# Splitting GpSimd's three wide rounding steps into halves, and planning with other durations, in a one-core transformer layer

## The reference

```python
x = x + attention(layernorm(x), Wq, bq, Wk, bk, Wv, bv, Wo, bo)   # x: 2 x 2048 x 256, 16 heads of 16, causal, rope
x = x + ffn(layernorm(x), w_gate, w_up, w_down)                    # inner width 704

def fp4_quant_dequant(x):            # blocks of 16 along the last dim
    scale = max(max(abs(block)) / 6, 1e-12)
    return grid(block / scale) * sign * scale      # grid 0, .5, 1, 1.5, 2, 3, 4, 6
def fp4_linear(x, w): return fp4_quant_dequant(x) @ fp4_quant_dequant(w).T
def ffn(x):           return fp4_linear(silu(fp4_linear(x, w_gate)) * fp4_linear(x, w_up), w_down)
```

## Time and profile before

| what | before |
|---|---|
| median of 3 runs | 1327.4 us (1326.84 to 1329.7) |
| the profiled execution | 1327.12 us, its span 1324.8 us |
| PE busy | 1235.4 us, 93% of the span |
| DVE busy | 1079.2 us, 81% |
| ACT busy | 773.1 us, 58% |
| POOL busy | 474.7 us, 36% |

### The profile page before, as it was taken

One profiled execution on the slowest core, in us unless ns is written; L12 is line 12 of the kernel. 1 busy time (PEld: TensorE's weight loads), 2 busy tenths in 40 slices (PEclk: granted clock), 3 DMA queues, 4 the chain that ended last, 5 costly groups with the idle time before them and its releaser, 6 DMA issues.

```text
span 1324.8 us, 43878 instructions
## 1 busy us (share of the span) xinstructions
PE 1235.4 (93%) x18934; PEld 712.9 (54%) x18934; DVE 1079.2 (81%) x2434; ACT 773.1 (58%) x1659; POOL 474.7 (36%) x500
## 2 busy tenths in 40 slices
PE   7568899999999999999989899999999999999967
PEld 6445555554555545555546655555555546545445
DVE  5778988978988899899618788899899898994356
ACT  5335566655656446567675456557566585776621
POOL 2956625645231131311106554313213121023346
PEclk9778999999999999999999999999999999999979
DMA  4623322222011000110122312120111100000000
GB/s 107 169 75 103 86 70 58 66 65 58 11 33 35 26 18 11 33 26 11 36 65 59 89 42 58 42 51 10 35 34 35 35 2 19 3 3 17 14 13 16
DMA packets 63901, 57.54 MB, mean 43 GB/s; under 512 B 17359, under 2 KB 57297, under 8 KB 63697
## 3 DMA queue, kind: packets, MB, share of 16 engines
q1 hardware_dynamic: 60680, 53.67, 15.4%
q10 hardware_dynamic: 3028, 1.09, 0.3%
HBM read 37.55 MB, written 16.78 MB: 41 GB/s over the span
## 4 chain that ended last, share of the span: by engine, by line
PE 71%; DVE 16%; POOL 5%; issue 3%; ACT 3%; DMA 2%; SPq 0%; ACTq 0%; POOLq 0%; DVEq 0%
PE bank L911 16%; PE bank L865 14%; PE bank L887 14%; PE bank L923 11%; DVE piece_max L1270 6%; PE bank L1036 5%; PE bank L983 3%; ACT prob L1172 2%; PE bank L1027 2%; PE bank L991 1%; PE bank L918 1%; DVE c_mem L1347 1%; PE bank L998 1%; PE bank L892 1%; DVE c_mem L1337 1%
## 5 line engine op out<-in xcount | busy, mean ns | idle before, releaser
L1172 ACT ACTIVATE prob<-bank 128x512 f32<-128x512 f32 (+3 forms) x1280 | 603.7, 539 | 272.8 <-PE bank L887 150.6
L1270 DVE TENSOR_REDUCE piece_max<-bank 128x1 f32<-128x512 f32 (+14 forms) x1280 | 675.6, 579 | 26.5 <-PE bank L865 13.6
L887 PE MATMUL bank<-q_mem,k_mem 99*32 99x512 bf16 (+15 forms) x5120 | 397.6, 341 | 8.6 <-DVE piece_max L1270 5.2
L865 PE MATMUL bank<-k_mem,q_mem 96*32 96x512 bf16 (+14 forms) x5120 | 388.5, 343 | 6.7 <-DVE piece_max L1270 4.3
L911 PE MATMUL bank<-prob,V 128*32 128x512 f32 (+3 forms) x2560 | 296.2, 534 | 12.2 <-ACT prob L1172 11.7
L1484 POOL TENSOR_TENSOR c_mem<-c_mem 128x256 f32<-128x256 f32 (+2 forms) x74 | 86.4, 1168 | 443.8 <-DVE c_mem L1359 443.8
L887 PEld LDWEIGHTS bank<-q_mem,k_mem 99*32 99x32 bf16 x5120 | 144.6, 96 | 159.1 <-issue 77.3
L865 PEld LDWEIGHTS bank<-k_mem,q_mem 96*32 96x32 bf16 x5120 | 143.4, 97 | 144.7 <-issue 81.8
L892 PE MATMUL bank<-mask_kq,ident_h 128*32 128x128 bf16 (+3 forms) x2048 | 104.8, 201 | 0.0
L911 PEld LDWEIGHTS bank<-prob,V 128*32 128x32 f32 x2560 | 67.8, 110 | 63.6 <-ACT prob L1172 26.3
L870 PE MATMUL bank<-mask_qk,ident_h 128*32 128x32 bf16 x2048 | 93.9, 182 | 0.0
(11 more groups left out here) (173 smaller groups left out, 1390.1 us busy)
## 6 DMA issues: line engine op xcount, KB each, us to landing
parts_dram<-a_mem SPq DMA_DIRECT2D x13, 512.0 KB, 4.0
q_mem<-parts_dram SPq DMA_DIRECT2D x32, 192.0 KB, 3.0
k_mem<-parts_dram SPq DMA_DIRECT2D x32, 192.0 KB, 3.5
q_mem<-parts_dram SPq DMA_DIRECT2D x32, 128.0 KB, 3.0
k_mem<-parts_dram SPq DMA_DIRECT2D x32, 128.0 KB, 3.4
c_mem<-in_L_attn_x SPq DMA_DIRECT2D x30, 128.0 KB, 2.1
out<-c_mem SPq DMA_DIRECT2D x30, 128.0 KB, 1.7
a_mem<-in_L_attn_x SPq DMA_DIRECT2D x13, 256.0 KB, 3.0
```

What stands on the lines that cost most here:

```text
L865: m = pe.matmul(b[COLUMNS * h:COLUMNS * (h + 1), of], q_rows(u)[0:TERM_ROWS, h, block * COLUMNS:(block + 1) * COLUMNS], k_rows(k0 // CHUNK ...
L887: mm = pe.matmul(b[k0:k0 + COLUMNS, since:CHUNK], k_rows(j // TPC, g)[:, h, first:first + COLUMNS], q_rows(u)[:, h, since:CHUNK], start=Tr ...
L1172: act.activation(prob[:, n % NP, off:CHUNK], bank_of("st", n)[:, off:CHUNK], ACT.Exp, scale=SCALE).then_inc(drained("st", n)[0], 1)
L1270: r = dve.tensor_reduce(piece_max[:, u % 2, block, slot:slot + 1], bank_of("s1", n)[:, column:column + keys], AX.X, ALU.max)
```

## The change

GpSimd's three rounding steps on rows of 704 become six, each on a half of 352 numbers, ordered add/add, subtract/subtract, multiply/multiply. Rows of 256 stay whole. What TensorE waits for is still the last of them. Two waits move: the q matmuls wait for q's weight alone and the k matmuls for k's (both waited for both), and in rope the step that overwrites the memory which the v matmuls still read comes third, so that the first two steps do not wait for v. All else alters only the planner's assumptions, and through them the order of the streams.

```diff
-DMA_TURN_NS, DMA_NS, DMA_KB_PER_NS, DIVIDE_NS, BESIDE_NS = 460, 1500, 0.2, 96, 2000
-SOONER_NS = dict(a=0, w=0, xn=10000, s=200, st=0, pv=-100, place=1000, norm=200, c=(0, -2000), tile=1000)
+DMA_TURN_NS, DMA_NS, DMA_KB_PER_NS, DIVIDE_NS, JOIN_NS, BESIDE_NS = 460, 1500, 0.2, 96, 150, 2500
+SOONER_NS = dict(a=0, w=0, xn=10000, s=200, st=0, pv=-1000, place=10000, norm=200, c=(0, -2000), tile=1000)
...
         if engine == "pe" and divided != self.divided:
-            ns, self.divided = ns + DIVIDE_NS, divided
+            ns, self.divided = ns + (DIVIDE_NS if divided else JOIN_NS), divided
...
+        if engine == "pool" and self.sharing[0] <= begin < self.sharing[1]:
+            ns += self.sharing[1] - begin
+        if shares:
+            self.sharing = begin, begin + ns
...
-        for n, ns in enumerate((whole, 85, blocks / 2, whole, whole / 2, whole / 2)):
-            yield from plan.step("dve", ("round", n) + key, ns, last, shares=n in (1, 4, 5))
+        for n, ns in enumerate((whole, 90, 62 + 0.39 * width, whole, whole / 2 + 36, whole / 2 + 36)):
+            yield from plan.step("dve", ("round", n) + key, ns, last, shares=n in (1, 3, 4, 5))
...
-        for n in range(3):
-            yield from plan.step("pool", ("grid", n) + key, 150 + (2.1 if n < 2 else 1.7) * width, last)
+        halves = grid_halves(width)          # 2 for rows of 704, else 1
+        for n, half in itertools.product(range(3), range(halves)):
+            yield from plan.step("pool", ("grid", n, half) + key, 150 + (2.1 if n < 2 else 1.7) * width / halves,
+                                 [("grid", n - 1, half) + key] if n else last)
...
             def project_features(b, z, o):
-                for s in range(2):
-                    at.wait_ge(*drained("aw", s))
+                at.wait_ge(*drained("aw", o))
...
-            at.wait_ge(*filled("v", z))
-            engine.tensor_tensor(to[:, :, 0], qk[:, :, 0], cos, ALU.mult).then_inc(done, 1)
-            yield when["rope1", z]
...
             engine.tensor_tensor(temp[:, 0], qk[:, :, 1], sin, ALU.mult).then_inc(done, 1)
+            yield when["rope1", z]
+            engine.tensor_tensor(temp[:, 1], qk[:, :, 0], sin, ALU.mult).then_inc(done, 1)
             yield when["rope2", z]
+            at.wait_ge(*filled("v", z))
+            engine.tensor_tensor(to[:, :, 0], qk[:, :, 0], cos, ALU.mult).then_inc(done, 1)
...
+                for n, half in itertools.product(range(3), range(halves)):
+                    at_, of = slice(half * each, (half + 1) * each), slice(half * nb, (half + 1) * nb)
+                    a, b, to = v["qa"][0:rows, at_], v["qb"][0:rows, at_], dst[:, at_]
+                    yield when[("grid", n, half) + key]
+                    if n == 0:
+                        at.wait_ge(*rounded)
+                        pool.tensor_tensor(a, a, b, ALU.add).then_inc(done, 1)
+                    elif n == 1:
+                        at.wait_ge(done, first + half + 1)
+                        pool.tensor_tensor(a, a, b, ALU.subtract).then_inc(done, 1)
+                    else:
+                        at.wait_ge(done, first + halves + half + 1)
+                        pool.tensor_tensor(...)      # multiply by the blocks' scales
```

More of the change, by code:

```diff
@@ L82, in __init__ @@
         self.spare, self.bank_free = list(banks), {b: 0.0 for b in banks}
-        self.jobs, self.now, self.running, self.moved, self.divided = [], 0.0, None, 0.0, False
+        self.jobs, self.now, self.running, self.moved = [], 0.0, None, 0.0
+        self.divided, self.sharing = False, (0.0, 0.0)
     def start(self, job, sooner=0.0):
@@ L306, in rehearse_projection @@
         for o, name in enumerate(("q", "k")):
[L307 to L308 removed]
+            plan.start(plan.through((name, z), 1728, "act", 360,
+                                    [("drain", "xnT", z), ("drain", "aw", o)],
                                     [("drain", "bias")] + old("lo"),
[L310 removed]
+                                    ("act", (name + "0", z), 372, ("drain", "bias"), *old("lo"))), pair_sooner(z))
         plan.start(plan.through(("v", z), 1728, "dve", 600, [("drain", "xnT", z), ("drain", "aw", 2)],
@@ L317, in rehearse_projection @@
         rope, ns = ("dve", 600) if rope_on_vector(z) else ("pool", 1235)
-        for n, after in enumerate(([("drain", "q", z), ("drain", "k", z), ("drain", "table", z), ("v", z)], old("stored", len(STORES) - 1),
-                                   [], [], [("rope1", z)], [("rope3", z)])):
-            yield from plan.step(rope, (f"rope{n}", z), ns, after)
+        for n, after in enumerate(([("drain", "q", z), ("drain", "k", z), ("drain", "table", z)] + old("stored", len(STORES) - 1),
+                                   [], [("v", z)], [], [("rope2", z)], [("rope3", z)])):
+            yield from plan.step(rope, (f"rope{n}", z), ns, after, shares=rope == "dve")
         yield from plan.step("act", ("hi", z), 960, [("rope5", z)])
-        yield from plan.step(rope, ("rest", z), 1130 if rope_on_vector(z) else 2200, [("hi", z)])
+        yield from plan.step(rope, ("rest", z), 1130 if rope_on_vector(z) else 2120, [("hi", z)], shares=rope == "dve")
         plan.start(rehearse_parts(z), pair_sooner(z))
@@ L330, in rehearse_low_part @@
     def rehearse_low_part(z):
[L331 removed]
+        yield from plan.step("dve", ("lo", z), 1135, [("mid", z)], shares=True)
         for n in range(1, len(STORES)):
@@ L433, in rehearse_weights @@
                 yield from rehearse_rounding(("w", n), width, ready)
-                ready = [("grid", 2, "w", n)]
+                ready = [("grid", 2, grid_halves(width) - 1, "w", n)]
             for part in range(weight_parts[n]):
-                yield from plan.through(("fw", n, part), 330, "act", 480, ready + [("ident load",)])
+                yield from plan.through(("fw", n, part), 330, "act", 300 + 190 * (name == "d" and part == 0), ready + [("ident load",)])
                 yield from plan.wait([("drain", "fw", n, part)])
```

72 lines of the change are left out of this document (30 added, 42 removed).

## The result

The changed kernel takes 1312.2 us (median of 4 runs, 1310.8 to 1314.0) where the kernel before takes 1327.1 us (4 runs, 1326.5 to 1329.7): the ratio is 0.9883, with a 95% interval of 0.9870 to 0.9895. That is 15 us less, where 7.6 us less were forecast. The direction is right and the time lies in the range, but the gain is twice the one that was forecast, so the working has to be gone through term by term. The profiled execution took 1312.96 us with a span of 1311.2 us; before it was 1324.8.

A forecast was written before the change was run, and what follows sets the result against it. TensorE was taken as nine tenths busy or more in nearly all of the middle, with holes at both ends. Terms -1.3 - 0.9 - 3.4 - 2.0 = -7.6 us took 1327.4 to 1319.8 us, range 1309 to 1330.

The forecast's parts named there:

- The end: Last tiles' chain: VectorE waits less behind halved GpSimd steps, 1.95 us back less 0.67 for the halves: -1.3 us.
- the price of the halves: GpSimd's wide roundings: six half steps cost 0.67 us more than three whole ones, 0.53 by spacing of starts.
- Rope: At the start, VectorE's first two rope steps run ahead of v's matmuls: -0.9 us.
- The moved waits of the weights: First q matmul, at the start: the wait for the k weight may cost at most 0.3 us, counted as nothing.
- The placing: First unit, before its second pass: fewer row maxima between its steps, -3.4 us; first exponential before 82.
- The mode changes: TensorE's full stretch: 20 fewer of 334 changes at 0.10 us each, -2.0 us.
- the values product's bias: TensorE's values product yields to scores up to 1 us younger; counted as nothing, hidden by TensorE's queue.
- the other assumed durations: Planner's durations: change only the order, which can't be priced; counted as nothing, they widen the range.
- Starved weights: Rival, at the start: sooner placing delays the weights' rounding and TensorE waits, +6.0 us, 1333; chance 0.17.
- Start repaired: Rival: better durations remove two of TensorE's three waits for weights, -17.8 us at most, some 1311; chance 0.16.
- GpSimd held up: Rival, last three tiles: VectorE gets in at the halves' new borders, the end gives +3.2, 1324.3 us; chance 0.08.
- GpSimd busy 497 us: Sign over the whole kernel: 34 wide roundings at 0.67 us make GpSimd busy 23 us more, 497 us.

The follow-up runs named there:

- e1: The changed kernel with its planned order kept, GpSimd's three wide steps emitted whole where their first halves stood: 1318.5 us, ratio 0.9944.
- e12: The kernel before in its own order, with GpSimd's three wide steps cut into halves in place: 1327.9 us, ratio 0.9989.
- e7: The kernel before with only the three new biases (BESIDE_NS 2500, pv -1000, place 10000): 1308.4 us, ratio 0.9850.
- e16: The order of e7, with GpSimd's wide steps cut into halves in place: 1309.2 us, ratio 0.9848 against the kernel before.
- e17: The changed kernel with the biases whose plan had the earliest rehearsed end of 300 (BESIDE_NS 2750, pv -1000, place 1000, s 250): 1290.6 us, ratio 0.9707.
- e8: The changed kernel with all three biases set back to their old values: 1338.1 us, ratio 1.0074 against the kernel before.
- e11: The kernel before with BESIDE_NS at 2050 instead of 2000, a change that means nothing: 1344.0 us, ratio 1.0121.
- e5: The changed kernel with 151 added two-column matmuls of the whole array in the first pass, 574 mode changes: 1368.8 us, ratio 1.0297.
- e6: Control for e5: the changed kernel with four tiny strip matmuls at each of the same 151 places, 302 mode changes: 1313.6 us, ratio 0.9889.

## Why the prediction was half right

- **The end, -1.3.** The mechanism is right: VectorE waits for the rest of a shorter step, and at a fixed order the end gains 1.8 us (e1) or 2.3 us (e12). Mis-sized was the price of the halves, 0.19 us a rounding for 0.67: -1.95 + 0.19 = -1.8. The prediction came nearest with 0.53, where it took start-to-start spacing into account. But the kernel's end gained nothing, 63.4 to 63.7 us, since the new order of the last tiles gave back about 2 us (e1's 65.5 against 63.4). I had reckoned the end in the old order's chain, and there left out the c_mem tile between the two k_mem tiles, whose lines 1347 and 1355 (1.66 and 1.28 us) lie on it too.
- **Rope, -0.9.** The start moved from 19.73 to 18.84, as forecast, but the sixth step ends only 0.24 us sooner and the first store is no sooner. The term counted the start and not what VectorE puts in between. It was not tried alone, and rope's first step starts anywhere from 18.6 to 20.3 us in the kernels of the old type, so 0.9 us of one execution say little.
- **The moved waits of the weights, 0.** q's matmuls start at 11.87 us, ahead of the second weight's transposes, instead of at 13.04; k's last drain starts at 18.24 instead of 18.27. Nothing came of it, as forecast; not tried alone.
- **The placing, -3.4.** 8.7 us instead of 7.5, so 2.3 us gained there; the first exponential at 77.2 met its mark of 82. The loss in the first 100 us fell by 1.7 to 2.8 us, where 4.3 were forecast for rope and placing together. Sixes of row maxima became twos, but two of VectorE's steps on 16 numbers still took 1.32 and 2.09 us.
- **The mode changes, -2.0.** 32 fewer instead of 20, at a confirmed 0.10 us: 3.2 us. A right price, a number too low.
- **The step that failed** is the sentence beside it: the values product's bias counted nothing, "hidden by TensorE's own queue", and "the other assumed durations change only the order, which I can't price; they count nothing and widen the range". The middle was worth -12 us where the sum had -2.0. With the three biases alone, at the old durations and with whole steps, e7 gains 20 us, more than the whole change and far more than the 5.4 us that the sum gave to placing and mode changes: the order, which the sum put at nothing, was its largest term. About 3 of the 12 us are mode changes; by e1 some 2.5 are the halves in this order (e12 and e16 show that the same halves give nothing there in two others); the rest is not taken apart by a run. Fewer waits for exponentials are among it (9 for 20 in the middle), longer waits for the placed maxima stand against it (6.5 us for 1.0). The shares of the parts stay open, since the moved waits and the durations were not run alone. I had read a middle at nine tenths as full. It had 36.0 us of holes in 1100 us, and more loss beside them: room for what e17 found.
- **The rivals.** Starved weights: no, the wait of line 944 shrank. Start repaired: two of the three waits did vanish, as that rival had it, and the time, 1312.2, is near its 1311; but the start gained 1.7 to 2.8 us, not 10, because 6.3 us of waits for the placed maxima and the row maxima came up in the same stretch. The right time would have come from the wrong reason. GpSimd held up: hardly. A held step shows as a longer step and not as idle time. In the kernel after, each of the three roundings ahead of the very last has a pair of multiplies of 2.2 us, where the last pair, with nothing to hold it, takes 1.53; in the kernel before, two of the three whole multiplies take 1.91 for 1.39. That is 0.65 us a tile for 0.52, and not the 1.5 of this rival.
- **GpSimd busy 497 us.** 485.3. e1 with whole steps has 471.2, so the halves add 14 us where 23 were forecast from prices alone; in e12, on the old order, 488.6 against 474.7, again 14. The halves were not dearer than forecast by their own length (933 to 939 ns an add for 955); they overlap, and the gap between dependent steps is gone, so the price of a rounding is 0.19 us from end to end and 14 / 34 = 0.41 in busy time, which does not count the old gaps.

What stays open: which stalls combine in a given order to make it 10 us better than its neighbour. The waits for exponentials, the mode changes and the placing are each seen to move, and none alone follows the time over all runs. The rehearsed end follows it within a type, which says that the planner's model holds much of the answer, not what the answer is. The new assumed durations were not run without the biases and the halves; that they cost time with old biases is read from e8, where all but the biases is together. The lines through 8 and 5 points have seen one test each.

## What to carry to other kernels

Where a planner lays the order from constants, price an edit in two parts: its work at a fixed order (put the new instructions into the old plan, as e12), and the draw of a new order, which here moved the time by up to 16 us for constants that meant nothing, as much as a good optimisation. Never credit a constant for one run's gain: run a neighbour that means nothing (e11) first. And if a plan's own rehearsed end follows the measured times of a few orders, with the same assumed durations in all of them, search hundreds of plans by it and run the best; that gave 22 us beyond the change under study. Lastly, price GpSimd's steps from first start to last end; adding up their spans had a price of 0.19 us at 0.67.

## What the runs showed of the hardware

- A change between 32-wide strips and the whole array on TensorE costs 0.09 us out of the whole array (0.110 to 0.202 between the starts of transposes, 80 changes) and 0.11 us back into it (0.218 to 0.326 for scores, 40 changes), in the trace of the kernel after; 272 added changes (e5 against e6) bound it between 0.06 and 0.11.
- A VectorE step on 44 numbers (line 1353 of e1), 181 ns when GpSimd is idle, ends 41 to 48 ns behind the GpSimd step in which it starts, 12 times of 12, and so takes up to 1676 ns. In the last 35 us it took 1456 ns beside steps of 704 numbers (e1) and 431 beside steps of 352 (after), two steps each. VectorE's reductions and reciprocals are not held (0.88 and 0.42 us in both cases).
- Two GpSimd steps that depend on each other leave 0.07 us between them; independent halves leave none and their spans overlap. Three steps on 704 numbers take 4.92 us from first start to last end (before), six on 352 take 5.10 (after).
